# Graph attention on one core: one-hots, transposes and their copies made two groups ahead of the products instead of one

## The chip, the cores and the metric

The kernel runs on one core of a Trainium2 chip. The metric is the time on the device in microseconds (us); the median of three runs is given, and one further execution was profiled. A group below is four tiles of 128 edges each, a window is eight groups.

## The reference

One layer of graph attention over 6250 nodes and 206250 edges, which come sorted by receiver, then a residual and a layer norm:

```python
sent = nodes[senders] @ Ws + Ws_b
e_att = sent + edges @ We + We_b
recv = nodes[receivers] @ Wr + Wr_b
logits = einsum('ehd,do->eho', mish(e_att + recv), attn_w) + attn_b
seg_max = segment_max(logits, receivers)
w = exp(logits - seg_max[receivers])
w = w / segment_sum(w, receivers)[receivers]
out_nodes = segment_sum(w * e_att, receivers)
x = layernorm(x + out_nodes)
```

There are 4 heads of 32, so 128 features. All data are float32.

## The kernel before

The edges are cut into W = 51 windows of 4096 (128 partitions times T = 32 tiles). In a window the receivers span at most 128 nodes, so a sum over receivers is a matrix product with a one-hot of 128 columns. Tables of the nodes' sender and receiver projections are made first and stored to DRAM. Then each engine runs its own loop over windows and, in them, over NG = 8 groups of GT = 4 tiles. The windows from 2 to 49 are a loop of two windows a turn; two buffers (b) hold the data of even and odd windows.

For group g of window w:

- VectorE, `one_hots` (L1073): the one-hot of the group's local receivers (L1077). It writes the buffer of two windows back, so it waits for the sums of the same group of window w-2 (L1075).
- TensorE, `turn` (L761): four transposes of the edges (L768) into the one PSUM tile `ps_edgeT` and four of the one-hot, as bf16 (L773), into the one `ps_onehotT`. The first wait for ScalarE's copy of the group before (L766), the second for `one_hots` and that copy's pair (L770, L771).
- ScalarE, `copy_edgeT` (L878, L883) and `copy_onehotT` (L885, L890): copies of the two to SBUF, into one of two buffers (g % 2), each after the products of two groups back.
- TensorE, `products` (L777): for each tile edges times We (L787) plus one-hot times the receivers' rows (L788), added up in `ps_z`, 16 instructions a group, since a float32 matmul is two. They wait for both copies and for the addition of two groups back.
- GpSimd, `gathers` (L693, L699): for each tile an indirect DMA that fetches 128 rows of the senders' table, 4 a group. Those of a group start when the addition of the group four back is done (AHEAD = 4, L697).
- VectorE, `add_gathered` (L1082, L1088): products plus gathered rows into Z, "the addition". Then `clamp` (L1096); ScalarE's four steps exp, square, ln, exp (L897, L900, L903, L907); and on VectorE, a group later, `mish` (L1103), `score` (L1112) and `reduce_heads` (L1118), which give the logits.

When a window's logits are there, its maxima are found in the next window (L1121 to L1168), the weights are made, `messages` (L1174, L1179) multiplies them into Z, and `sums` on TensorE (L792, L799) adds up the messages over receivers with the one-hots as stationary operand, eight instructions a group. The tables MSG_NEXT, MSG_LAST (messages) and SUM_NEXT, SUM_LAST (sums) say in which group of the next or next but one window each is issued: SUM_NEXT = {5: [0], 6: [1], 7: [2]} in the next, SUM_LAST = {1: [3, 4], 2: [5, 6], 3: [7]} in the one after it. `attended`, `moments` and `normalise` finish a window two windows later and SyncE stores it. `prepare` (L1052) makes the local receivers (part 1, L1057, L1059) and the penalties (part 2) of the next window in group 6.

The engines run independently and each in its own order. In a group g VectorE does: one-hots of g+1, addition of g, messages, clamp of g, mish, score and reduction of g-1, and small work between them. TensorE does: products of g, transposes of g+1, sums. ScalarE does: copies of g+1, the four steps of g. SyncE, in order: edge load, receivers, receiver indices, sender indices (after the gathers), store and residual rows of finished windows; the edge load waits for the last edge transposes of two windows back (L607).

Of the kernel before, what the change touches and what calls it, by code (L numbers as in the profile page):

```python
# [51 lines left out]
SUM_NEXT = {5: [0], 6: [1], 7: [2]}  # L52
SUM_LAST = {1: [3, 4], 2: [5, 6], 3: [7]}
NCONST = 3
# [13 lines left out]
def gat_kernel(nc, x, src, dst, edges, ws_k, ws_b, wr_k, wr_b, we_k, we_b, attn_w, attn_b, out):  # L68
# [13 lines left out]
    with ctx:  # L82
# [217 lines left out]
        def after(w, b, g):  # L300

            return (w, b, g + 1) if g + 1 < NG else (w + 1, 1 - b, 0)

        def before(w, b, g):
            return (w, b, g - 1) if g else (w - 1, 1 - b, NG - 1)

        def run(eng, window):

            window(0, 0, 0)
            window(1, 1, 0)  # L310
            with eng.Fori(1, W // 2) as i:
                window(i * 2, 0, i)
                window(i * 2 + 1, 1, i)
            window(W - 1, 0, W // 2)
            window(W, 1, W // 2)
            window(W + 1, 0, W // 2 + 1)
# [403 lines left out]
        def _(pe):  # L720
# [96 lines left out]
            def window(w, b, k):  # L817
                for g in range(NG):
                    if there(w):
                        products(w, b, k, g)  # L820
                    w1, b1, g1 = after(w, b, g)
                    if there(w1) and there(w):
# [12 lines left out]
            pe.wait_ge(s_xs, 2 * NB)  # L835
            turn(0, 0, 0, 0)
            run(pe, window)
            pe.wait_ge(fin, (W - 1) * FIN)
# [7 lines left out]
        def _(act):  # L846
# [82 lines left out]
            def window(w, b, k):  # L929
                for g in range(NG):  # L930
                    w1, b1, g1 = after(w, b, g)
                    here, coming = there(w), there(w1) and there(w)
# [16 lines left out]

            copy_edgeT(0, 0, 0)  # L950
            copy_onehotT(0, 0, 0)
            run(act, window)
# [4 lines left out]
        def _(dve):  # L957
# [279 lines left out]
            def aside(w, b, k, g, part):  # L1237

                if g == 3 and there(w - 1):
                    subtract_maxima(w - 1, 1 - b, part)  # L1240
                if g == 4 and there(w - 2):
                    attended(w - 2, b, k - 1, part)
                if g == 5 and there(w - 2):
                    moments(w - 2, b, k - 1, part)
                if g == 6 and there(w + 1) and there(w):
                    prepare(w + 1, 1 - b, k + b if b else k, part)
# [7 lines left out]
            def window(w, b, k):  # L1254


                for g in range(NG):
                    w1, b1, g1 = after(w, b, g)
                    w0, b0, g0 = before(w, b, g)
# [32 lines left out]
            dve.wait_ge(prep_row, 1)  # L1292
            one_hots(0, 0, 0)
            look_for_unsorted()
            run(dve, window)
# [25 lines left out]
```

## Time and profile before

| what | value |
|---|---|
| median of three runs | 2827.16 us (2823.28 to 2833.03) |
| profiled execution | 2829.57 us, its span 2827.6 us |
| mean granted clock of TensorE | 0.848 |
| instructions in the span | 45501 |
| mean DMA rate | 85 GB/s |

The profile's page gives the busy time of each engine, the idle time before each group of instructions and what ended it. "Remote" in it means that the semaphore that ended a wait rose at a moment near which no recorded instruction of the program ended; the kernel runs on one core, so it is no other core. "Issue" is idle time in which an engine waited for nothing that the profile shows. The granted clock is a share of 2.4 GHz; it has two levels here, 0.50 and 1.00.

### The profile page before, as it was taken

What the parts mean: (1) busy time and instruction counts of PE and PEld (TensorE: products, weight loads), DVE (VectorE), ACT (ScalarE), POOL (GpSimd) and SP (SyncE); (2) the same over time, 40 slices, a digit from 0 to 9 for tenths busy, and PEclk for the clock granted to TensorE, in tenths of its full rate; (3) what the DMA queues carried; (4) which work ended last, traced back from release to release, by engine and by line L of the source; (5) the groups of instructions that cost most, each with busy time, mean ns of one, the idle gap of its engine ahead of it and who ended that gap; (6) DMA issues with size and microseconds to landing.
All of it is one profiled execution on the core that took longest, in us unless ns stands there. A gap on an engine that the chain in (4) does not pass through costs nothing.

```text
span 2827.6 us, 45501 instructions
## 1 busy us (share of the span) xinstructions
PE 1930.7 (68%) x13618; PEld 1782.6 (63%) x13618; DVE 2032.6 (72%) x4348; ACT 1634.8 (58%) x2717; POOL 1555.1 (55%) x1640
## 2 busy tenths in 40 slices
PE   4566777667676676676667676677666666767666
PEld 4566666666666666666666666666566666666665
DVE  3577777777777777767777777777777677777776
ACT  1556555556565665565655656655656556656663
POOL 2555555555555555555555555555555555555551
PEclk9788788888888888888887988888988789888888
DMA  6322322322322322232232232232232232232220
GB/s 198 105 71 75 107 74 74 107 73 73 108 71 73 99 82 72 77 101 73 75 104 75 75 105 75 76 104 75 75 105 74 72 106 73 73 103 76 74 77 17
DMA packets 107468, 240.30 MB, mean 85 GB/s; under 512 B 46429, under 2 KB 73300, under 8 KB 100412
## 3 DMA queue, kind: packets, MB, share of 16 engines
q0 software_dynamic: 52224, 107.06, 14.4%
q1 hardware_dynamic: 53074, 132.41, 13.7%
q10 hardware_dynamic: 2142, 0.49, 0.1%
q8 instruction: 13, 0.21, 0.0%
q14 instruction: 15, 0.12, 0.0%
HBM read 230.09 MB, written 9.74 MB: 85 GB/s over the span
## 4 chain that ended last, share of the span: by engine, by line
DVE 35%; PE 24%; another core or an unknown queue 18%; issue 16%; ACT 4%; DVEq 1%; ACTq 1%; SPq 0%; DMA 0%
PE ps_z L787 7%; PE ps_z L788 7%; DVE tbuf L1112 6%; DVE Z L1088 5%; DVE tbuf L1103 5%; DVE onehot L1077 5%; PE ps_sum L799 4%; DVE Z L1179 4%; DVE tbuf L1096 3%; DVE logit L1118 2%; PE ps_onehotT L773 2%; PE ps_edgeT L768 1%; ACT tbuf L900 1%; ACT tbuf L897 1%
## 5 line engine op out<-in xcount | busy, mean ns | idle before, releaser
L699 POOL DMA_INDIRECT gath<-xs_table,src_i x1632 | 1554.2, 952 | 1218.6 <-DVE Z L1088 652.5
L787 PE MATMUL ps_z<-we_sb,edgeT 128*128 128x128 f32 x3264 | 800.3, 334 | 575.2 <-ACT edgeT L883 316.5
L787 PEld LDWEIGHTS ps_z<-we_sb,edgeT 128*128 128x128 f32 x3264 | 622.6, 237 | 629.2 <-ACT edgeT L883 345.7
L788 PE MATMUL ps_z<-xr_buf,onehotT 128*128 128x128 f32 x3264 | 768.6, 324 | 4.2 <-issue 4.2
L1088 DVE TENSOR_TENSOR Z<-ps_z,gath 128x512 f32<-128x512 f32 x408 | 279.9, 686 | 553.5 <-remote 399.4
L788 PEld LDWEIGHTS ps_z<-xr_buf,onehotT 128*128 128x128 f32 x3264 | 630.5, 240 | 4.1 <-issue 4.1
L883 ACT COPY edgeT<-ps_edgeT 128x512 f32<-128x512 f32 x408 | 238.4, 584 | 668.6 <-remote 463.7
L799 PE MATMUL ps_sum<-Z,onehot 128*128 128x132 f32 x3264 | 491.1, 300 | 37.6 <-issue 32.7
L799 PEld LDWEIGHTS ps_sum<-Z,onehot 128*128 128x128 f32 x3264 | 440.9, 209 | 42.1 <-issue 37.3
L890 ACT CAST onehotT<-ps_onehotT 128x512 f32<-128x512 bf16 x408 | 239.7, 588 | 199.7 <-remote 135.3
L1077 DVE TENSOR_TENSOR onehot<-iota_f,ps_dve 128x512 f32<-128x512 f32 x408 | 272.8, 669 | 100.3 <-remote 100.3
L897 ACT ACTIVATE tbuf<-tbuf 128x512 f32<-128x512 f32 x408 | 257.8, 632 | 123.9 <-DVE tbuf L1096 80.4
L773 PE MATMUL ps_onehotT<-ident_half,onehot 128*128 128x128 bf16 x1632 | 180.3, 238 | 212.1 <-DVE onehot L1077 126.2
L768 PE MATMUL ps_edgeT<-ident,edge_buf 128*128 128x128 f32 x1632 | 296.5, 308 | 27.1 <-issue 20.9
L900 ACT ACTIVATE tbuf<-tbuf,c_one 128x512 f32<-128x512 f32 x408 | 294.6, 722 | 13.3
L903 ACT ACTIVATE tbuf<-tbuf,c_one 128x512 f32<-128x512 f32 x408 | 294.6, 722 | 13.3
L773 PEld LDWEIGHTS ps_onehotT<-ident_half,onehot 128*128 128x128 bf16 x1632 | 118.6, 107 | 283.9 <-DVE onehot L1077 167.8
L907 ACT ACTIVATE ps_ratio<-tbuf,c_ln 128x512 f32<-128x512 f32 x408 | 281.3, 689 | 17.1 <-ACT tbuf L903 2.1
L1112 DVE TENSOR_TENSOR tbuf<-tbuf,ps_dve 128x512 f32<-128x512 f32 x408 | 278.4, 682 | 7.3
L1118 DVE TENSOR_REDUCE logit<-tbuf 128x16 f32<-128x512 f32 x408 | 277.7, 681 | 7.3
L1103 DVE SCALAR_TENSOR_TENSOR tbuf<-ps_ratio,Z 128x512 f32<-128x512 f32 x408 | 277.7, 681 | 0.0
L1179 DVE TENSOR_TENSOR Z<-Z,ps_dve 128x512 f32<-128x512 f32 x408 | 272.1, 678 | 1.8
(107 smaller groups left out, 1131.0 us busy)
## 6 DMA issues: line engine op xcount, KB each, us to landing
edge_buf<-in_edge_attr_dram SPq DMA_DIRECT2D x51, 2048.0 KB
gath<-xs_table,src_i POOLq DMA_INDIRECT x1632
xr_buf<-xr_table SPq DMA_DIRECT2D x51, 64.0 KB
xr_in<-xr_table SPq DMA_DIRECT2D x51, 64.0 KB
x_in<-in_x_dram SPq DMA_DIRECT2D x51, 64.0 KB
out_dram<-y_out SPq DMA_DIRECT2D x51, 64.0 KB
xs_table<-onehot SPq DMA_DIRECT2D x2, 896.0 KB
xr_table<-Z SPq DMA_DIRECT2D x1, 1568.0 KB
```

What stands on the lines that cost most here:

```text
L699: nc.gpsimd.indirect_dma_start(gath[:, b, t, :], None, xs_dram, bass.IndirectOffsetOnAxis(ap=src_i[:, b, t:t + 1], axis=0))\
L768: tr = nc.tensor.transpose(ps_edgeT[:, j, :], edge_buf[:, b, a + j, :], ident[:, :])
L773: tr = nc.tensor.transpose(ps_onehotT[:, j, :].bitcast(BF16)[:, 0:P], halves(OHv[:, b, a + j, :]), ident_half[:, :])
L787: nc.tensor.matmul(ps_z[q][:, j, :], edgeT[:, q, j, :], we_sb[:, :], start=True, stop=False)
L788: mm = nc.tensor.matmul(ps_z[q][:, j, :], onehotT[:, q, j, :], xr_buf[:, b, :], start=False, stop=True)
L799: mm = nc.tensor.matmul(ps_sum[:, 0:ZC], OHv[:, b, t, :], Zv[:, b, t, :], start=(t == 0), stop=(t == T - 1))
L1077: nc.vector.tensor_tensor(OHv[:, b, a:a + n, :], iota_f[:, :].unsqueeze(1).to_broadcast([P, n, P]), local[:, b, a:a + n].unsqueeze(2).to_b ...
L1088: nc.vector.tensor_tensor(Zv[:, b, a:a + n, 0:D], ps_z[g % 2][:, 0:n, :], gath[:, b, a:a + n, :], ALU.add).then_inc(z_ready, 1)
L1103: nc.vector.scalar_tensor_tensor(out=tb, in0=ratio, scalar=1.0, in1=Zv[:, b, a:a + n, 0:D], op0=ALU.subtract, op1=ALU.mult, reverse0=True)\
L1112: nc.vector.tensor_tensor(tb, tb, row.to_broadcast([P, n, D]), ALU.mult).then_inc(scored, 1)
L1118: nc.vector.tensor_reduce(logit[:, b, :, a:a + n].rearrange("p h t -> p t h"), tb, AX.X, ALU.add)\
L1179: nc.vector.tensor_tensor(zz, zz, ww, ALU.mult).then_inc(msg_ready, 1)
```

## The change

One-hots, transposes and copies are issued for the group two ahead of the products: `two_after` takes the place of `after` on VectorE, TensorE and ScalarE, and a second group of each is made before the loop. The sums of the window two back move one group sooner: 3 and 4 to group 0, 5 to group 1, 6 to group 2; 7 stays in group 3. Part 1 of `prepare` moves from group 6 to group 5, since the one-hots of the next window's first group now come at the head of group 6. Buffers, GpSimd and SyncE are as before.

```diff
-SUM_LAST = {1: [3, 4], 2: [5, 6], 3: [7]}
+SUM_LAST = {0: [3, 4], 1: [5], 2: [6], 3: [7]}
...
+        def two_after(w, b, g):
+
+            return after(*after(w, b, g))
+
...
                 for g in range(NG):
                     if there(w):
                         products(w, b, k, g)
-                    w1, b1, g1 = after(w, b, g)
+                    w1, b1, g1 = two_after(w, b, g)
                     if there(w1) and there(w):
                         turn(w1, b1, k if w1 is w else (k + b if b else k), g1)
...
             turn(0, 0, 0, 0)
+            turn(0, 0, 0, 1)
             run(pe, window)
...
                 for g in range(NG):
-                    w1, b1, g1 = after(w, b, g)
+                    w1, b1, g1 = two_after(w, b, g)
                     here, coming = there(w), there(w1) and there(w)
                     if coming:
                         copy_edgeT(w1, b1, g1)
...
-            copy_edgeT(0, 0, 0)
-            copy_onehotT(0, 0, 0)
+            for g in range(2):
+                copy_edgeT(0, 0, g)
+                copy_onehotT(0, 0, g)
...
-                if g == 6 and there(w + 1) and there(w):
+                if (g, part) in ((5, 1), (6, 2)) and there(w + 1) and there(w):
                     prepare(w + 1, 1 - b, k + b if b else k, part)
...
-                    w1, b1, g1 = after(w, b, g)
+                    w1, b1, g1 = two_after(w, b, g)
                     w0, b0, g0 = before(w, b, g)
                     if there(w1) and there(w):
                         one_hots(w1, b1, g1)
...
             one_hots(0, 0, 0)
+            one_hots(0, 0, 1)
             look_for_unsorted()
```

## Rows read from the trace of the kernel before

**Rows 1.** The page, part 1: busy us, share of the span, instructions

```profile
PE 1930.7 (68%) x13618; PEld 1782.6 (63%) x13618; DVE 2032.6 (72%) x4348; ACT 1634.8 (58%) x2717; POOL 1555.1 (55%) x1640
```

**Rows 2.** The addition's line: ns min/median/max, first and last start

```profile
L1088 DVE TENSOR_TENSOR Z<-ps_z,gath x408: 671/691/693, 78.0 to 2789.5; 128x512 f32<-128x512 f32 x136
```

**Rows 3.** Table of waits: who <- what ended it: us, times, longest

```profile
DVE Z L1088 <- remote: 399.4, 137, 4.9
...
PE ps_z L787 <- ACT edgeT L883: 316.5, 119, 5.1
...
DVE Z L1088 <- PE ps_z L788: 143.4, 66, 7.2
...
DVE onehot L1077 <- remote: 100.3, 28, 4.0
```

**Rows 4.** Timeline of TensorE's matmuls: start, us, line, names, count [idle before]

```profile
1398.65 1.12 PE L799 MATMUL ps_sum<-Z,onehot 128*128 128x132 f32 x8
1399.61 0.39 PE L787 MATMUL ps_z<-we_sb,edgeT 128*128 128x128 f32 x2
...
1401.17 0.39 PE L788 MATMUL ps_z<-xr_buf,onehotT 128*128 128x128 f32 x2
...
1406.65 0.35 PE L799 MATMUL ps_sum<-Z,onehot 128*128 128x132 f32 x1 [0.45 <-issue]
1408.34 0.77 PE L787 MATMUL ps_z<-we_sb,edgeT 128*128 128x128 f32 x2 [1.34 <-ACT onehotT L890]
```

**Rows 5.** Timeline of VectorE and ScalarE from the anchor at 1406.80

```profile
1406.80 0.69 DVE L1088 TENSOR_TENSOR Z<-ps_z,gath 128x512 f32<-128x512 f32 x1 [3.71 <-remote]
1406.93 0.59 ACT L883 COPY edgeT<-ps_edgeT 128x512 f32<-128x512 f32 x1 [3.68 <-remote]
...
1410.63 0.68 DVE L1077 TENSOR_TENSOR onehot<-iota_f,ps_dve 128x512 f32<-128x512 f32 x1
...
1412.13 0.69 DVE L1088 TENSOR_TENSOR Z<-ps_z,gath 128x512 f32<-128x512 f32 x1 [0.83 <-issue]
...
1416.92 0.59 ACT L890 CAST onehotT<-ps_onehotT 128x512 f32<-128x512 bf16 x1 [3.34 <-remote]
...
1421.06 0.69 DVE L1088 TENSOR_TENSOR Z<-ps_z,gath 128x512 f32<-128x512 f32 x1 [3.44 <-PE ps_z L788]
```

**Rows 6.** Timeline of GpSimd: eight gathers and the first of the next

```profile
1395.17 0.97 POOL L699 DMA_INDIRECT gath<-xs_table,src_i  x1 [3.24 <-DVE Z L1088]
...
1404.07 0.94 POOL L699 DMA_INDIRECT gath<-xs_table,src_i  x1 [0.30 <-issue]
1408.27 0.96 POOL L699 DMA_INDIRECT gath<-xs_table,src_i  x1 [3.25 <-DVE Z L1088]
```

**Rows 7.** Timeline of VectorE: a one-hot's wait at group 2, and anchors

```profile
1143.56 0.69 DVE L1088 TENSOR_TENSOR Z<-ps_z,gath 128x512 f32<-128x512 f32 x1 [3.96 <-remote]
...
1156.59 0.69 DVE L1077 TENSOR_TENSOR onehot<-iota_f,ps_dve 128x512 f32<-128x512 f32 x1 [3.96 <-remote]
1157.19 0.68 DVE L1088 TENSOR_TENSOR Z<-ps_z,gath 128x512 f32<-128x512 f32 x1
...
1164.42 0.69 DVE L1088 TENSOR_TENSOR Z<-ps_z,gath 128x512 f32<-128x512 f32 x1 [1.23 <-PE ps_z L788]
...
1393.69 0.69 DVE L1088 TENSOR_TENSOR Z<-ps_z,gath 128x512 f32<-128x512 f32 x1 [2.30 <-PE ps_z L788]
```

**Rows 8.** Stretch of products, busy us of PE, PEld, DVE, ACT, POOL; clock, DMA

```profile
1408.30:1412.10 3.80, 3.76 (x17) 3.79 (x18) 2.94 (x6) 2.77 (x4) 2.88 (x4) 0.50 0.16 43
```

**Rows 9.** Groups by line: names, count | busy us, mean ns | idle before

```profile
L1077 DVE TENSOR_TENSOR onehot<-iota_f,ps_dve 128x512 f32<-128x512 f32 x408 | 272.8, 669 | 100.3 <-remote 100.3
...
L1103 DVE SCALAR_TENSOR_TENSOR tbuf<-ps_ratio,Z 128x512 f32<-128x512 f32 x408 | 277.7, 681 | 0.0
...
L1096 DVE TENSOR_SCALAR tbuf<-Z 128x512 f32<-128x512 f32 x408 | 179.7, 440 | 2.1
```

**Rows 10.** Timeline of VectorE: the first operation of prepare, part 1

```profile
1400.41 0.24 DVE L1057 TENSOR_SCALAR ps_dve<-dst_i,base_f 128x32 f32<-128x32 int32 x1
```

**Rows 11.** SyncE's own waits: line <- what: us, times, longest

```profile
SPq L294 <- DVE y_out L1225: 244.5, 10, 45.3
```

## What I expect, and why

> **What bounds the kernel now.** I read the page first. No engine is full: VectorE 2032.6 us of a span of 2827.6, TensorE 1930.7, ScalarE 1634.8, GpSimd 1555.1 [rows 1]. Per group of four tiles (408 of them) that is 4.98, 4.73, 4.01 and 3.81 us, while a group takes 6.66 us: the additions into Z run from 78.0 to 2789.5, 407 steps in 2711.5 us [rows 2]. So the kernel is bound by waits, and the table of waits says which: VectorE's additions for "remote" (399.4 us) and for the products (143.4), TensorE's products for ScalarE's copies (316.5), VectorE's one-hots for "remote" (100.3) [rows 3]. "Remote" on one core means here that a semaphore rose and no instruction of the program had its recorded end near that moment.
>
> The timeline shows what it is. The products of the group that is added at 1406.80 have their last record from 1401.17 for 0.39 us [rows 4]; the addition that needs only them and a long landed gather starts at 1406.80 after 3.71 us idle, and ScalarE's copy of the transposes behind those products at 1406.93, after 3.68 [rows 5]. TensorE's results become known to others about 5 us after their record. GpSimd's timeline gives the pattern [rows 6]: the addition at 1393.69 lets gathers start at 1395.17; eight are issued, until 1405.01, and 1.79 us later the held results come free. 1.48 + 9.84 + 1.79 = 13.11 us, the distance of the additions at 1393.69 [rows 7] and 1406.80 [rows 5]. The first addition of such a cycle frees four gathers, the second one four more, the third is held until they are through. So the basic loop is VectorE's addition, eight gathers, TensorE's held update, and it does two groups in 13.1 us: 6.55 each. I call the additions that end a hold anchors.
>
> Here a page speaks against reading this as a hold. The Trainium skill, "Perfetto Trace Analysis", section "Per-engine timelines", says that TensorE's end time is computed by the profiler from an instruction's size and not observed. By it TensorE could really be computing until 1406.7, its bound would be its own work, and reordering would bring nothing; that is the rival "nothing moves" below. The trace leaves it open, though the last sum before 1406.8 stands alone behind 0.45 us of idle for nothing the profile shows [rows 4], which fits a TensorE that is stopped more than one that works.
>
> **The change part by part.** No instruction is added or removed: 408 one-hots, pairs of copies and sets of transposes stay. They move.
>
> 1. *Copies two groups ahead.* Now TensorE's order is products(g), transposes(g+1), sums, products(g+1), and products(g+1) stand behind ScalarE's copies of g+1: 2 x 0.59 us and, after an anchor, a start at 1408.34 where the addition was at 1406.80 [rows 4, 5]. Then they run at a granted clock of 0.50, the 1.2 GHz level, and last until the next addition at 1412.13 [rows 5, 8], 3.8 us and 5.33 after the anchor; those from 1399.61 to 1401.56 took 2.0 [rows 4]. After the change products(g+1) have their copies from a group before. Their other wait (Z two back) is unchanged, and copy(g+2) now waits for products(g), which stand ahead of its transposes anyway: nothing. But the gain is capped: VectorE comes to the second addition by itself about 4.4 us after the first (wide operations of 0.68 and a clamp of 0.44 [rows 9]; the one-hot starts 3.83 after the anchor and takes 0.67 at most, 1410.63 against 1406.80 [rows 5]), and the second four gathers cannot start before the first four are issued, 1.48 + 10.1/2 = 6.5 after the anchor. At a regular anchor the gain is 0; what can be gained is where the second addition comes too late and GpSimd's eight break into four and four, as from 1157.19 to 1164.42, 7.23 us for one group [rows 7], or where copies are themselves held, as that of 1416.92 with the addition then at 1421.06 behind 3.44 us idle [rows 5].
>  The whole that irregular cycles cost is 2711.5 - 407 x 6.55 = 45.6 us. Ends: 0 and 45.6 gained.
>
> 2. *The wait at group 2.* VectorE's one-hot of group 3 stands at the head of group 2, and needs the sums of the same group two windows back, which TensorE makes in group 1, only one group earlier. They fall into the hold: 28 one-hots waited, 100.3 us [rows 3]. The price is not 100: at 1156.59 the one-hot waited 3.96 us and the addition followed at 1157.19 with no wait [rows 7]; without it the addition itself would have waited to 1156.6. So 0.60 each, 28 x 0.60 = 17 us, part of the 45.6. With the new table these sums come in group 0: gone.
>
> 3. *New waits of the same kind.* This is what speaks against the change. One-hots now stand two groups ahead. Counting which group makes the sum and which needs it (one-hots of 0, 1 at groups 6, 7 and of 2, 3 at groups 0, 1; sums 0, 1, 2 at 5, 6, 7, sum 3 at 0): the distance is one group at four places, 6, 7, 0 and 1, where now it is one at group 2 alone. The other four have two. In the windows from 1143 to 1412 five anchors at these places wait 3.7 us or more for a held update, of 20 places (first 1143.56, last 1406.80, five in all) [rows 5, 7]. 5/20 x 204 = 51 new events at 0.60 = 31 us. A sum that is done before the hold costs 0 (lower end); all places twice per window and with a broken pair behind each (7.23 against 6.55 per group, 0.68) is 102 x 1.28 = 131 (upper end). I take 31, the row of the same wait.
>  Who stands behind such a wait: on VectorE the addition; on TensorE the onehot transposes, and behind them, in order, the sums and the products that were to run ahead. At these anchors part 1 brings nothing.
>
> 4. *Sums one group sooner.* Each is eight instructions in 1.12 us [rows 4]. Their messages are made at least one group ahead in both tables, so they wait for nothing new. Groups 1 and 2 held two each; now group 0 holds two and the others one: moved, 0, between plus and minus one sum (1.12) at an anchor, within part 3's ends.
>
> 5. *prepare, part 1, at group 5* instead of 6: two small operations, the larger 0.24 us [rows 10], moved, 0; at an anchor they lie in its wait, elsewhere they would cost up to 0.5 x 51 = 24. At the start one more one-hot stands ahead of the search, 0.67 us [rows 9]: 0 to 0.7.
>
> 6. *SyncE's queue.* The 2 MB edge load waits for the last edge transposes of two windows back, which come a group sooner. It is held by the store ahead of it, which waits for the normalised rows (244.5 us on that) [rows 11], so it does not move: 0. If it moved a group (6.6 us) it would meet other gathers; bounds plus and minus 3 us a window where it shows, which I leave to the range.
>
> **Sum.** 2829.6 (the profiled execution; its span is 2827.6) - 45.6 + 31 = 2815. The median of the three runs is 2827.2, 2.4 below it, so 2813 to 2815; I say 2814, 0.5% faster. I take the whole 45.6 because the two things that are seen to break cycles, late products and the wait at group 2, are what the change moves.
>
> **The rivals.**
> - *The new waits win* (slower). Mechanism: at 6, 7, 0 and 1 the one-hot waits for held sums, TensorE stands behind it and goes on at the lower clock, and the next products come so late that the eight gathers break into four and four. For: the same wait at group 2 did just that: 1156.59, then 1157.19 to 1164.42 [rows 7]. Against: only group 0 has two sums ahead of the products. Price 1.28 each; with no gain of part 1 but the 17 of part 2, 51 events give 2827 + 65 - 17 = 2875; with half the gain of part 1, 2860; with a third of the places, 2840. Middle 2850. It decides from 45.6 / 1.28 = 36 events on, where each costs the full price.
> - *Nothing moves*. The loop of addition, eight gathers and held update contains none of the moved parts; or TensorE really works until the update. Then 2827 plus or minus 8.
> - *Three groups fit into a cycle*: with products ahead, the third addition is known before the hold begins, and twelve gathers follow each other. (1.48 + 14.9 + 1.79) / 3 = 6.06 a group, 0.5 less; in a third of the 407 steps that is 67 us: 2760. Against: TensorE waits with the transposes of g+3 for a one-hot that VectorE starts 3.83 us after the anchor, and only behind them and a sum come the products of g+2: 3.83 + 0.67 + 0.2 + 1.12 + 2.0 = 7.8 us after it [rows 4, 5], when the record of the hold of 1406.80 had long begun (its products ended 1401.56, 7.9 after 1393.69).
> - *The change does not reach its distance*: TensorE still stops at the edge transposes of g+2 until the copy of g+1 has freed the one buffer. It is part of "nothing moves".
>
> **How the numbers follow.** Forecast (2795 to 2820) 0.38; new waits win 0.34; nothing moves 0.22; three groups 0.06. The range should leave out 2 in 10: it takes the forecast, nothing moves, and the slower case to 2868, and down to 2770: **2770 to 2868**. The likeliest case's own range is 2795 to 2820. A measurement here tells 0.3% (8.5 us) from no change. Faster by more than that 0.42, within 0.22, slower 0.36.
>
> **What would show it.** Right: the additions of regular anchors still 13.1 apart; the idle time of the one-hots for "remote" no longer at group 2 but at 6, 7, 0 and 1, some 50 times; TensorE's products waiting for the copy of edgeT far less than 316.5 us; the additions' wait for ps_z below 143.4. Wrong: one-hots with over 70 such waits, more pairs 7.2 apart, or bursts of twelve gathers (faster). The sum is wrong at its root if the hold is no matter of the gathers: then anchors would not come 1.8 us behind the last gather's issue.

## The result, and the profile after

The kernel after takes 2771.8 us (median of 4 runs, 2766.4 to 2773.1), the kernel before beside it 2830.1 (4 runs, 2823.3 to 2839.2): ratio 0.9763, 95% interval 0.9728 to 0.9797. That is 2.4% faster. The forecast was 2814 us, 0.5% faster; the direction was right, the size was not: of the 58 us gained, 13 were foreseen (2827.2 to 2814), under a quarter. The time lies 2 us inside the stated range of 2770 to 2868, and outside 2795 to 2820, the likeliest case's own. The profiled execution has a span of 2764.5 us at a granted clock of 0.866.

The page's part 1 of the kernel after:

```profile
PE 1889.1 (68%) x13618; PEld 1751.4 (63%) x13618; DVE 2027.6 (73%) x4348; ACT 1631.1 (59%) x2717; POOL 1570.5 (57%) x1640
```

The busy times are those of before [rows 1] within 16 us, TensorE aside (42 less, at a slightly higher clock). The kernel is still bound by waits. The tables of waits of VectorE, TensorE and GpSimd (who <- what ended it: us, times, longest), and the line of the addition with its first and last start:

```profile
DVE Z L1094 <- remote: 620.9, 199, 5.7
...
DVE Z L1094 <- PE ps_z L792: 14.9, 17, 3.8
...
DVE onehot L1083 <- remote: 7.4, 4, 4.0
...
PE ps_onehotT L777 <- DVE onehot L1083: 357.8, 180, 4.0
PE ps_onehotT L777 <- issue: 265.6, 125, 5.1
PE ps_sum L803 <- issue: 92.1, 141, 1.7
...
POOL gath L703 <- DVE Z L1094: 659.7, 208, 10.4
...
L1094 DVE TENSOR_TENSOR Z<-ps_z,gath x408: 659/691/693, 76.9 to 2728.7; 128x512 f32<-128x512 f32 x136
```

Against [rows 3]: the products' wait for ScalarE's copies, 316.5 us, is gone; so are the additions' waits for products (143.4, now 14.9) and the one-hots' (100.3, now 7.4). What came in their place is the hold itself: additions wait for "remote" 199 times where they did 137 times, that is at nearly every second of the 408 groups. GpSimd's timeline tells what that means for its bursts (gathers with less than 1 us between them): 196 are of eight, 3 of four and 3 of twelve; of the kernel before 152 were of eight and 100 of four. Nearly every cycle is now the regular pair.

The arithmetic closes. The additions run 2728.7 - 76.9 = 2651.8 us, where they ran 2711.5 [rows 2]: 59.7 less; what lies outside took 116.1 and takes 112.7: 3.4 less; together the 63.1 between the spans.

A regular cycle of the kernel after on VectorE (timeline, one-hots and additions):

```profile
1363.44 0.69 DVE L1094 TENSOR_TENSOR Z<-ps_z,gath 128x512 f32<-128x512 f32 x1 [3.01 <-remote]
...
1367.69 0.66 DVE L1083 TENSOR_TENSOR onehot<-iota_f,ps_dve 128x512 f32<-128x512 f32 x1
1368.27 0.68 DVE L1094 TENSOR_TENSOR Z<-ps_z,gath 128x512 f32<-128x512 f32 x1
...
1372.28 0.68 DVE L1083 TENSOR_TENSOR onehot<-iota_f,ps_dve 128x512 f32<-128x512 f32 x1
1376.41 0.69 DVE L1094 TENSOR_TENSOR Z<-ps_z,gath 128x512 f32<-128x512 f32 x1 [3.45 <-remote]
...
1380.24 0.68 DVE L1083 TENSOR_TENSOR onehot<-iota_f,ps_dve 128x512 f32<-128x512 f32 x1
```

The additions of 1363.44 (group 5) and 1376.41 (group 7) end holds, 12.97 apart; the one between needs no wait, since its products had their copies a group before. GpSimd's first gather of the cycle is at 1364.92 and the eighth ends at 1374.72. TensorE in the same cycle (timeline of matmuls):

```profile
1368.41 0.40 PE L777 MATMUL ps_onehotT<-ident_half,onehot 128*128 128x128 bf16 x4 [3.02 <-DVE onehot L1083]
1368.64 1.12 PE L803 MATMUL ps_sum<-Z,onehot 128*128 128x132 f32 x8
1369.60 0.38 PE L791 MATMUL ps_z<-we_sb,edgeT 128*128 128x128 f32 x2
...
1371.16 0.39 PE L792 MATMUL ps_z<-xr_buf,onehotT 128*128 128x128 f32 x2
...
1374.21 0.27 PE L791 MATMUL ps_z<-we_sb,edgeT 128*128 128x128 f32 x1
1374.88 0.35 PE L791 MATMUL ps_z<-we_sb,edgeT 128*128 128x128 f32 x1 [0.40 <-issue]
1376.28 0.39 PE L792 MATMUL ps_z<-xr_buf,onehotT 128*128 128x128 f32 x2 [1.05 <-issue]
```

Two things are to be seen. The sum that the one-hot of 1372.28 needs is made from 1368.64, directly behind the transposes, 4.8 us after the burst's first gather when it ends; it was known in time. The products behind it, recorded until 1371.55, 6.6 us after it, were not: their addition is that of 1376.41. And behind 1374.21 TensorE has one product at a time with idle time for "issue" between them, until the hold ends at 1376.4: it does not only tell late what it has done, it is itself stopped. All sixteen records of that group's products are in the trace, so no missing record fills the gaps.

### The profile page after: what moved, and what is told of

Read it like the earlier page. It is cut to its first block, busy times and chain, and to the rows that moved or that the text cites. A ratio compares the mean times of both kernels' runs of the same rounds, so it can differ in the third digit from the quotient of the medians.

```text
span 2764.5 us, 45477 instructions
## 1 busy us (share of the span) xinstructions
PE 1889.1 (68%) x13618; PEld 1751.4 (63%) x13618; DVE 2027.6 (73%) x4348; ACT 1631.1 (59%) x2717; POOL 1570.5 (57%) x1640
## 3 DMA queue, kind: packets, MB, share of 16 engines
q0 software_dynamic: 52224, 107.06, 14.9%
## 4 chain that ended last, share of the span: by engine, by line
DVE 51%; another core or an unknown queue 21%; issue 16%; PE 9%; DVEq 1%; ACTq 1%; ACT 1%
DVE Z L1094 8%; DVE onehot L1083 8%; DVE tbuf L1118 8%; DVE tbuf L1109 7%; DVE Z L1185 6%; DVE tbuf L1102 4%; DVE logit L1124 3%; PE ps_sum L803 3%; PE ps_z L791 2%; PE ps_z L792 2%; DVE ends_max L1159 1%; DVE item_pen L1145 1%; PE ps_onehotT L777 1%; PE ps_edgeT L772 1%
## 5 line engine op out<-in xcount | busy, mean ns | idle before, releaser
L791 PE MATMUL ps_z<-we_sb,edgeT 128*128 128x128 f32 x3264 | 760.5, 319 | 38.3 <-issue 37.7
L792 PE MATMUL ps_z<-xr_buf,onehotT 128*128 128x128 f32 x3264 | 744.0, 313 | 47.1 <-issue 46.7
L791 PEld LDWEIGHTS ps_z<-we_sb,edgeT 128*128 128x128 f32 x3264 | 608.3, 231 | 52.9 <-issue 49.9
L803 PE MATMUL ps_sum<-Z,onehot 128*128 128x132 f32 x3264 | 571.0, 323 | 100.7 <-issue 92.1
L792 PEld LDWEIGHTS ps_z<-xr_buf,onehotT 128*128 128x128 f32 x3264 | 604.1, 229 | 54.7 <-issue 53.2
L777 PE MATMUL ps_onehotT<-ident_half,onehot 128*128 128x128 bf16 x1632 | 171.4, 231 | 630.8 <-DVE onehot L1083 357.8
L803 PEld LDWEIGHTS ps_sum<-Z,onehot 128*128 128x128 f32 x3264 | 493.2, 226 | 118.0 <-issue 109.5
L777 PEld LDWEIGHTS ps_onehotT<-ident_half,onehot 128*128 128x128 bf16 x1632 | 105.7, 102 | 708.9 <-DVE onehot L1083 404.6
L912 ACT ACTIVATE ps_ratio<-tbuf,c_ln 128x512 f32<-128x512 f32 x408 | 281.2, 689 | 11.6
L772 PE MATMUL ps_edgeT<-ident,edge_buf 128*128 128x128 f32 x1632 | 261.7, 285 | 18.5 <-issue 12.7
```

Source lines behind the costliest of these rows:

```text
L777: tr = nc.tensor.transpose(ps_onehotT[:, j, :].bitcast(BF16)[:, 0:P], halves(OHv[:, b, a + j, :]), ident_half[:, :])
L791: nc.tensor.matmul(ps_z[q][:, j, :], edgeT[:, q, j, :], we_sb[:, :], start=True, stop=False)
L792: mm = nc.tensor.matmul(ps_z[q][:, j, :], onehotT[:, q, j, :], xr_buf[:, b, :], start=False, stop=True)
L803: mm = nc.tensor.matmul(ps_sum[:, 0:ZC], OHv[:, b, t, :], Zv[:, b, t, :], start=(t == 0), stop=(t == T - 1))
```

## The experiments

The runs were made in five sets, each with the kernel before beside it on the same chip. The kernel before took 2829.7 us in the first, 2184.9 in the second, 2186.4 in the third, 2759.8 in the fourth and 2847.6 in the fifth. All ratios are within a set. Each set ran on another chip and no chip was used twice, so a difference between sets can be one of the chip or of the moment; "chip" below stands for both.

**Set 1: the parts, and the gathers.** The sums' table alone, in the kernel before:

```diff
-SUM_LAST = {1: [3, 4], 2: [5, 6], 3: [7]}
+SUM_LAST = {0: [3, 4], 1: [5], 2: [6], 3: [7]}
```

> The kernel before with the new table of sums alone (3 and 4 in group 0, 5 in 1, 6 in 2). Theory A (the gain is that broken cycles became regular, and the wait of the one-hot at group 2 was what broke them): the 28 one-hot waits go, most of the 100 bursts of four gathers with them, and the time falls by 40 us or more, to 2790 or less. Theory B (it takes the greater distance of transposes and copies): the 28 waits of 0.60 us go, 17 us at most, 2810 to 2825, and bursts of four stay at 70 or more.

Measured: 2809.0 us, ratio 0.9928 (0.9894 to 0.9961). No one-hot waited, and GpSimd's timeline has 80 bursts of four instead of 100. That is theory B, 1 us below its bounds.

The kernel after with transposes and copies one group ahead as before:

```diff
-                    w1, b1, g1 = two_after(w, b, g)
+                    w1, b1, g1 = after(w, b, g)
...
-            turn(0, 0, 0, 1)
...
-            for g in range(2):
-                copy_edgeT(0, 0, g)
-                copy_onehotT(0, 0, g)
+            copy_edgeT(0, 0, 0)
+            copy_onehotT(0, 0, 0)
...
```

> The changed kernel with transposes and copies one group ahead again; one-hots stay two ahead, the sums in the new table. Theory A (VectorE's earlier one-hots free TensorE's transposes): as the changed kernel, 2765 to 2780, nearly all bursts of eight. Theory B (products must not stand behind ScalarE's copies of the group before): between the two, 2800 to 2830, TensorE's products still wait 200 us or more for the copy of edgeT.

Measured: 2828.2 us, ratio 1.0004 (0.9972 to 1.0036), theory B. Here are the waits that the prediction feared (table of waits, and VectorE's timeline):

```profile
DVE onehot L1081 <- remote: 315.3, 92, 4.7
...
PE ps_z L791 <- ACT edgeT L887: 219.6, 100, 5.1
...
1350.06 0.69 DVE L1081 TENSOR_TENSOR onehot<-iota_f,ps_dve 128x512 f32<-128x512 f32 x1 [4.01 <-remote]
1350.66 0.68 DVE L1092 TENSOR_TENSOR Z<-ps_z,gath 128x512 f32<-128x512 f32 x1
```

92 one-hots waited, all of groups 0 to 3 (made at groups 6, 7, 0 and 1), nearly twice the 51 forecast. With the copies' distance they are 4. So the parts do not add: the sums alone bring 21 us (11 to 30), one-hots and sums together nothing, and with the copies it was 58 in the first comparison. The copies' distance is what makes the earlier one-hots harmless.

Half the gathers, in the kernel before and in the kernel after: from the third window on only two of a group's four tiles are gathered, the other two keep what an earlier window left there, so the work of half the gathers is left out. The waits for landed gathers are halved to match.

```diff
-                    for t in range(a, a + n):
+                    few = n if isinstance(w, int) and w < 2 else n // 2
+                    for t in range(a, a + few):
...
```

> The kernel before with two gathers a group in place of four from the third window on (tiles 2 and 3 of a group add rows that an earlier window left). Theory of the held updates (the loop is addition, gathers, TensorE's updates set free when the gathers are through): the loop of two groups shrinks from 13.1 us to 1.5 + 5.0 + 1.5, 8 us, under VectorE's own 5.0 a group, so 2150 to 2400 us in all, VectorE bound. Rival (TensorE really computes until its late updates): no less work for TensorE, 2800 to 2830.

> The changed kernel with two gathers a group in place of four from the third window on (tiles 2 and 3 of a group add rows that an earlier window left). Held updates: VectorE bound, 2100 to 2350 us, and ahead of the kernel before with half its gathers by 50 us or more, since copies no longer stand between products. Rival (TensorE really computes): 2760 to 2775.

Measured: 2208.9 and 2211.4 us, ratios 0.782 and 0.783. TensorE, VectorE and ScalarE do the same work as ever, in 78% of the time. From the windows with half the gathers on, no addition waits for "remote" in either; the few that do start before 162 us, while four gathers a group are still made. So the loop that sets the time goes through the gathers. The second half of the last expectation failed: the change, said to be 50 us ahead here, is worth nothing, so its gain shows only where updates are held.

**Sets 2 and 3: the same kernels where nothing is held.** Four variants of the kernel after were to follow the cycle. An idle operation of GpSimd ahead of each group's gathers (128 columns); one of 512 columns with the gathers six groups ahead instead of four; the last sums one group apart from their one-hots; one-hots three groups ahead, behind the clamp:

```diff
...
+                    nc.gpsimd.iota(pad_i[:, :], pattern=[[1, 128]], base=0, channel_multiplier=0).then_inc(s_pad, 1)
...
```
```diff
-AHEAD = 4
+AHEAD = 6
...
+                    nc.gpsimd.iota(pad_i[:, :], pattern=[[1, 512]], base=0, channel_multiplier=0).then_inc(s_pad, 1)
```
```diff
-SUM_LAST = {0: [3, 4], 1: [5], 2: [6], 3: [7]}
+SUM_LAST = {0: [3], 1: [4], 2: [5, 6], 3: [7]}
```
```diff
-SUM_NEXT = {5: [0], 6: [1], 7: [2]}
-SUM_LAST = {0: [3, 4], 1: [5], 2: [6], 3: [7]}
+SUM_NEXT = {5: [0], 6: [1], 7: [2, 3]}
+SUM_LAST = {0: [4], 1: [5], 2: [6], 3: [7]}
...
-                if (g, part) in ((5, 1), (6, 2)) and there(w + 1) and there(w):
+                if (g, part) in ((4, 1), (6, 2)) and there(w + 1) and there(w):
...
-                    w1, b1, g1 = two_after(w, b, g)
+                    w1, b1, g1 = after(*two_after(w, b, g))
...
-                    if there(w1) and there(w):
-                        one_hots(w1, b1, g1)
...
+                    if there(w1) and there(w):
+                        one_hots(w1, b1, g1)
...
```

> The changed kernel with one small operation on GpSimd (an iota of 128 columns, 0.23 us in the profile of the kernel before, at L690) ahead of each group's four gathers. If the loop is addition, eight gathers, late updates, each of the 204 pairs gets two of them, 0.5 us at the least and 1.1 with 0.3 us of issue each: 2870 to 2990. If TensorE's own work were the bound, GpSimd has 40% idle and nothing moves: 2760 to 2780.

> The changed kernel with gathers up to six groups ahead and an iota of 512 columns (about 0.5 to 0.9 us) on GpSimd ahead of each group's four, so that no eight gathers run without a break. If a break of over 1 us each group is enough to let TensorE's updates through: 5.0 + 1.1 to 1.4 us a group, 2600 to 2720. If the engine must be idle for longer, or counts as busy in the iota: 13.1 + 2 x 0.8 us for two groups, 2900 to 3060.

> The changed kernel with the sums of the window two back as late as they can be: 3 in group 0, 4 in 1, 5 and 6 in 2, 7 in 3. The one-hots of groups 4 and 5 then also stand only one group behind their sums (six places of eight in place of four). The prediction's step 3 (a one-hot one group behind its sum meets a held update and costs 0.60 us): 30 to 60 us slower than the changed kernel, 2800 to 2830. If the regular cycle keeps the sums out of the held stretch, as the profile of the changed kernel shows with 7.4 us of such waits: within 8 us of it.

> The changed kernel with the one-hots three groups ahead, made behind the clamp, sum 3 in group 7 of the next window and 4 in group 0. TensorE's transposes then never wait for a one-hot, and the products two groups behind an anchor can be done 4 to 5.5 us after it, before updates are held. If that is what keeps a third group out of a cycle: many bursts of twelve gathers, 6.1 to 6.4 us a group, 2600 to 2730 us. If updates are held whatever is ready: 2760 to 2790.

Measured, in that order: 2214.8, 2338.4, 2171.6 and 2163.6 us; ratios 1.0136, 1.0699, 0.9929 and 0.9891, each within 0.002. None of the expected numbers could come, because the kernel before took 2184.9 us in this set: no addition waited for "remote" in any of the four. As tests of the held cycle they are void. The two with idle operations show something else, though. GpSimd's timeline of the first:

```profile
1362.46 0.94 POOL L708 DMA_INDIRECT gath<-xs_table,src_i  x1 [0.30 <-issue]
1363.40 0.26 POOL L706 IOTA pad_i<- 128x128 int32 x1
1363.82 0.95 POOL L708 DMA_INDIRECT gath<-xs_table,src_i  x1 [0.16 <-POOL pad_i L706]
```

From the fifth group on neither has a single pause of GpSimd longer than the 0.30 us of issue, over 1616 gathers. Gathers are 1.25 us apart; with the idle operation between them it is 1.36 in the first and 1.69 in the second (1364.99 to 1366.68), 0.11 and 0.44 more, over some 404 groups 44 and 178 us. Beside the three-ahead kernel of the same set, which has no pause of GpSimd either, they take 51 and 175 us more. What is added to GpSimd there comes out as time: where nothing is held, GpSimd's issuing sets the pace of these kernels.

So the change itself and three variants were run again, with an expectation for either case:

> The changed kernel itself, beside the kernel before, since the second set of runs found the kernel before at 2184.9 us where the first set had 2829.7: there no addition waited for "remote" and VectorE was busy for 93% of the span. Theory A (what the change is worth hangs on held TensorE updates): where the kernel before is near 2830, 2765 to 2780, ratio 0.976; where it is near 2185, the ratio is 0.993 to 1.003, 2170 to 2192, since VectorE's own work of 2025 us is the bound and only the products' wait for copies goes. Theory B (the change brings 2.4% by an order that is better anywhere): ratio 0.976 in both places, 2132 us beside 2185.

> One-hots and sums as in the change, transposes and copies one group ahead as before. In the first set this had 92 one-hots that waited (315 us idle) and was no faster than before, 2828.2. Theory A (it is held sums that make the one-hots wait): where the kernel before takes 2185, no one-hot waits (under 10 us), and the time is 2178 to 2195; where it takes 2830, 2820 to 2836 again. Theory B (the one-hots wait because TensorE's own order brings the sums too late): some 90 one-hots wait in both places, and it is over 2215 where the kernel before takes 2185.

> The changed kernel with its last sums at groups 0: 3, 1: 4, 2: 5 and 6, 3: 7, where the change has 0: 3 and 4, 1: 5, 2: 6, 3: 7. Sum 4 stands one group before the one-hot that needs it again, as in the kernel with new one-hots and old copies; only one sum stands ahead of the products at group 0. Theory A (with the copies two ahead, TensorE works early enough that every sum is known before a hold begins, so a one-hot does not wait): where the kernel before takes 2830, 2765 to 2785 and under 15 us idle of one-hots; where it takes 2185, 2168 to 2174. Theory B (the sums' table decides about the waits): over 30 one-hots wait, 2790 to 2820 where the kernel before takes 2830.

> The changed kernel with the one-hots three groups ahead (made behind the clamp), transposes and copies two ahead as in the change, sum 3 of a block one group sooner (in group 7 of the window after) and the first part of the preparation at group 4. Theory A (the held loop of addition, eight gathers, update takes 13.1 us and nothing in VectorE's order can shorten it): where the kernel before takes 2830, 2755 to 2785, the same as the change; where it takes 2185, 2158 to 2165 as measured before (2163.6). Theory B (the one-hot's place between hold and addition costs after each anchor, 0.67 us in 204 cycles, at least a fifth of it): under 2745 where the kernel before takes 2830.

The kernel before took 2186.4. Measured: the change 2187.4, ratio 1.0005 (0.9996 to 1.0015); one-hots and sums only 2167.0, 0.9915 (0.9898 to 0.9932); sums one apart 2170.4, 0.9927 (0.9910 to 0.9945); three ahead 2165.3, 0.9913 (0.9895 to 0.9931). For the change that is theory A, and for one-hots and sums only too as to the waits (none), though it is 11 us faster than its bounds; the other two came at theory A's times (three ahead at the upper bound). The change's page, part 1 and VectorE's row of busy tenths, then waits of VectorE, TensorE and GpSimd:

```profile
PE 1629.2 (75%) x13618; PEld 1523.9 (70%) x13618; DVE 2025.0 (93%) x4348; ACT 1634.0 (75%) x2717; POOL 1569.1 (72%) x1640
...
DVE  3799999999999999999999999999999999999997
```
```profile
DVE ends_max L1159 <- PE ps_ends L818: 58.3, 50, 1.8
...
DVE Z L1094 <- PE ps_z L792: 17.8, 21, 11.2
...
PE ps_onehotT L777 <- DVE onehot L1083: 500.2, 362, 3.4
...
POOL gath L703 <- issue: 472.3, 1538, 0.9
...
POOL gath L703 <- DVE Z L1094: 47.6, 93, 6.9
```

VectorE is busy for 93%, and GpSimd hardly pauses: its 72% leave out the 0.30 us of issue behind each gather, and among its last 1616 gathers only 29 pauses are longer than 0.45 us, 16 us in all beyond the issue. A group takes 5.09 us (2073.2 us of additions in 407 steps), four gathers 5.0. "Remote" is gone, and so are TensorE's idle times for "issue", of which the kernel after had 265.6 and 92.1 us at its transposes and sums where updates were held. GpSimd's gathers take what they took there, 962 and 961 ns each. The same program is bound by held updates on one chip and by GpSimd's and VectorE's own pace on another, 600 us apart, and the change is worth 2.4% on the first and nothing on the second. There the copies' distance even costs: the variant without it is 20 us faster. Its own waits:

```profile
POOL gath L703 <- issue: 472.7, 1551, 0.3
DVE Z L1092 <- DMA gath<-xs_table,src_i: 54.8, 47, 3.5
```

GpSimd has no pause left at all, and additions wait for gathers to land. VectorE's wait of `ends_max` for TensorE, 58.3 us in the change, is 1.0 here, and its busy time 2011.2 instead of 2025.0 (the clamp 176.6, 187.5). It would fit that these waits of VectorE make the 29 pauses in the change; no run tests it.

**Set 4: again with holds.** The three-ahead kernel and the one with sums one apart, as above:

> The same kernel as the one with one-hots three groups ahead, made behind the clamp, again: wanted is a set of runs in which the kernel before takes 2830. Theory A (what is lost after a hold is lost between the anchor's addition and the next one; the one-hot ahead of the second addition is 0.67 us of the 4.3 to 4.5 there, but the second four gathers can't start before the first four are issued, 6.2 us after the anchor): 2755 to 2785 there, additions of a regular cycle 13.0 to 13.2 apart. Theory B (sums and one-hots now fall into one group, and a sum made over 2 us after the burst's first gather is known only behind it, so the one-hot behind the clamp waits for it and with it the message and the scores): 2790 to 2850 there. Where the kernel before takes 2185: 2160 to 2168 again.

> The same kernel as the one with the last sums at 0: 3, 1: 4, 2: 5 and 6, 3: 7, again, for a set in which the kernel before takes 2830. Theory A (in the change anchors stand at groups 1, 3, 5, 7; a one-hot of an even group comes behind an addition that ended a hold, when everything is known, and one of an odd group needs a sum made just behind the one-hot of the group before, in the first 2 us of the burst, which are not held): this table moves only sum 4, needed at an even group, so no one-hot waits (under 15 us idle) and it takes 2765 to 2785. Theory B (one group between sum and one-hot is too little in general, and the change's table avoids it by luck of the place): over 30 one-hots wait, 2790 to 2820. Where the kernel before takes 2185: 2167 to 2174 again.

The kernel before took 2759.8. Three ahead: 2783.8, ratio 1.0091 (1.0075 to 1.0108). The bounds had been set for 2830; as ratios theory A's are 0.973 to 0.984 and theory B's 0.986 to 1.007, so it is B, and worse. One apart: 2733.3, ratio 0.9910 (0.9894 to 0.9927): no one-hot waited, as theory A has it, but the ratio is not within A's (0.977 to 0.984); it is within B's (0.986 to 0.996), for which over 30 one-hots were to wait. Neither theory holds whole. Here the held cycle is shorter (bursts of eight start 12.92 apart, 13.08 in the kernel after at first) and the kernel before loses less; the change itself was not run in this set. The table of waits of three ahead and one of its one-hots, with TensorE at the time:

```profile
DVE onehot L1083 <- remote: 220.5, 38, 7.8
...
1390.78 0.69 DVE L1083 TENSOR_TENSOR onehot<-iota_f,ps_dve 128x512 f32<-128x512 f32 x1 [7.68 <-remote]
```
```profile
1382.11 0.41 PE L791 MATMUL ps_z<-we_sb,edgeT 128*128 128x128 f32 x2
1382.99 0.27 PE L792 MATMUL ps_z<-xr_buf,onehotT 128*128 128x128 f32 x1 [0.47 <-issue]
1383.72 0.35 PE L792 MATMUL ps_z<-xr_buf,onehotT 128*128 128x128 f32 x1 [0.46 <-issue]
1385.80 0.27 PE L791 MATMUL ps_z<-we_sb,edgeT 128*128 128x128 f32 x1 [1.74 <-issue]
```

TensorE's two sums ahead of these products are recorded until 1381.38; the one-hot that needs one of them waited until 1390.78, 9.4 us after that. An order among the fastest where nothing is held (0.9891 and 0.9913) loses where updates are held.

**Set 5: a sum pushed into the hold.** The change itself; the change with twelve products of a zero matrix ahead of the sums of group 0; the same twelve behind them; and sums one apart, as in sets 2 to 4.

```diff
+                    if g == 0 and there(w - 2):
+                        for _ in range(12):
+                            nc.tensor.matmul(ps_sum[:, 0:P], zeros[:, :], ident[:, :], start=False, stop=False)
                     for m in SUM_LAST.get(g, []) if there(w - 2) else []:
                         sums(w - 2, b, m)
...
```

> The changed kernel, beside the two with idle products below and the table of sums one apart, so that all four stand on one chip. Both theories: on a chip that holds TensorE's updates, ratio 0.97 to 0.99 to the kernel before, with under 15 us idle of one-hots; where nothing is held, 1.000.

> The changed kernel with twelve products of a zero matrix added to the running sum, by TensorE in group 0 of each window, ahead of sums 3 and 4. The work grows by 12 x 51 products of some 0.14 to 0.3 us each, 1.7 us or more per window, in an engine that is idle 3 us per hold. In the change sum 3 was made 4.5 us (median) after a burst's first gather and known at once in 42 of 44 windows; updates 5 to 10 us after it are held. Theory A (the one-hots of odd groups don't wait because their sum is made just before the hold bites): where updates are held, sum 3 now falls into the hold and the one-hot at group 1 waits 3 to 4 us in most of 49 windows, 150 us or more in all; the addition follows 0.6 later at least: 30 to 60 us slower than the change. Theory B (the one-hots have room, the place of the sum in the cycle doesn't matter): within 8 us of the change. Where nothing is held: within 15 us of it.

> The same twelve idle products, but behind sums 3 and 4 of group 0: the same work in the same group, and sum 3 is as early as in the change. Theory A: no one-hot waits (under 15 us idle); the products of group 1 are 1.7 us or more later and are held anyway: within 8 us of the change. Theory B: the same time as the kernel with the idle products ahead of the sums, since only TensorE's work counts.

> The changed kernel with the last sums at 0: 3, 1: 4, 2: 5 and 6, 3: 7, beside the change itself: it moves one sum (about 1.1 us) out of group 0 and sum 6 stays in group 2. Theory A (the held cycle is addition, eight gathers, update, whatever stands in group 0): within 8 us of the change where updates are held. Theory B (fewer instructions ahead of the products of an anchor group bring its message and preparation sooner, as where nothing is held, 2170 beside 2187): 10 us or more faster than the change in both places.

Beside 2847.6 of before: the change 2780.6, ratio 0.9762 (0.9740 to 0.9785), as at first; idle ahead 2872.1, 1.0088 (1.0065 to 1.0111); idle behind 2883.7, 1.0123 (1.0096 to 1.0149); one apart 2774.4, 0.9738 (0.9717 to 0.9759).

The waits went as theory A has it (tables of waits, first of idle ahead, then of idle behind):

```profile
DVE Z L1101 <- remote: 453.5, 154, 6.4
DVE onehot L1090 <- remote: 175.4, 54, 4.3
DVE Z L1101 <- PE ps_z L794: 60.0, 53, 4.7
```
```profile
DVE Z L1101 <- remote: 432.4, 150, 6.3
DVE Z L1101 <- PE ps_z L794: 231.5, 58, 6.3
DVE onehot L1090 <- remote: 36.8, 17, 4.4
```

With the idle products ahead of sum 3 the one-hot that needs it waited over 1 us in 42 of 51 windows, behind it in 5. But theory A's times failed: the kernel with 37 more waits is the faster of the two by 11.6 us, and both are 91 and 103 slower than the change. A one-hot's wait inside a hold has, by this pair, no price that can be seen; the pair is no clean measure of it, since with the idle products behind the sums the additions wait 231.5 us for products, and 60.0 with them ahead. Theory B, the same time for both, is near, 11.6 us off, but has no place for the 42 waits. What has a price is TensorE's work in that group:

```profile
1378.23 1.73 PE L834 MATMUL ps_sum<-ident,zeros 128*128 128x128 f32 x14
1380.36 0.36 PE L834 MATMUL ps_sum<-ident,zeros 128*128 128x128 f32 x1 [0.40 <-issue]
1381.80 0.35 PE L834 MATMUL ps_sum<-ident,zeros 128*128 128x128 f32 x1 [1.08 <-issue]
1383.91 0.27 PE L834 MATMUL ps_sum<-ident,zeros 128*128 128x128 f32 x1 [1.76 <-issue]
1384.66 1.51 PE L834 MATMUL ps_sum<-ident,zeros 128*128 128x128 f32 x7 [0.48 <-issue]
1385.96 0.64 PE L793 MATMUL ps_z<-we_sb,edgeT 128*128 128x128 f32 x2
...
1384.74 0.69 DVE L1090 TENSOR_TENSOR onehot<-iota_f,ps_dve 128x512 f32<-128x512 f32 x1 [3.83 <-remote]
1389.14 0.69 DVE L1101 TENSOR_TENSOR Z<-ps_z,gath 128x512 f32<-128x512 f32 x1 [3.71 <-PE ps_z L794]
```

These are TensorE's and VectorE's timelines of the kernel with the idle products behind the sums; the twelve are 24 records (x). They wait for no semaphore. Between 1379.96 and 1384.66 TensorE does three records; then the rest at once, when the hold ends and the held one-hot starts too (1384.74). The products of group 1 come behind them, from 1385.96, and their addition waits for them until 1389.14; a one-hot's 0.60 after the hold's end it would have been 1385.3. What TensorE has not done when the hold begins, it does after it.

## Why the prediction was right or wrong

- **The loop** (addition, eight gathers, held update) stands where updates are held: 13.11 us was read, 13.08 is the median after, 12.97 in the cycle shown. With half the gathers the hold is gone, and with it over a fifth of the time. What the prediction took for an update that is told late is also an engine that is stopped.
- **Step 1, copies two ahead: the mechanism was right, the size too small.** Forecast 45.6 us with step 2 in it, the upper end; the loop lost 59.7. The 45.6 rest on 6.55 for half of 13.11; with 6.555 it is 43.6. Of the 14 more, 204 cycles at 13.08 instead of 13.11 are 6; the few bursts of twelve are part of the rest.
- **Step 2, the wait at group 2: right**, and measured by itself: 17 us forecast, 21 measured with the table alone (11 to 30 by its interval), which has no one-hot that waits.
- **Step 3, 51 new waits at 0.60, 31 us: this step failed.** There were 4, 7.4 us in all. The count was taken from the places where anchors stood in the kernel before, five of twenty, as if each anchor at such a place had the one-hot's wait ahead of it. (The whole trace has 37 additions there that waited 3.7 us or more for "remote", not 51, so by its own rule the term was 22.) In the regular cycle anchors stand at the odd groups. A one-hot of an even group (1380.24) comes behind an addition that ended a hold, when all is known; one of an odd group (1372.28) needs a sum that TensorE makes right behind the even group's transposes (1368.64), before it is stopped. The step counted events in the old pattern after step 1 had changed the pattern. Its own mechanism is real: without the copies' distance there were 92 waits, and with a sum pushed behind idle products 42 in one place alone. That part 1 "brings nothing" at such places was wrong in the same way. Its price of 0.60 found no support either: in set 5 the kernel with 37 waits more is the faster one, though the two differ in more than those waits.
- **Step 4, sums sooner: 0 within one sum per window.** Moving one sum out of group 0 gave 6.2 us (2780.6 to 2774.4), of overlapping intervals; but twelve idle products there cost 91 to 103. TensorE's idle time in the hold, which the expectations of set 5 counted on, is no cover: TensorE is stopped in it.
- **Steps 5 and 6** can't be told apart from nothing; outside the loop 3.4 us went.
- **The rivals.** "The new waits win" fell: the waits did not come. "Three groups fit" is 3 bursts of twelve, not a third. "The change does not reach its distance" fell: the products' wait for copies is gone. "Nothing moves" was right in set 3 (1.0005), for a reason that no rival had: nothing is held there. Its form from the Trainium skill, "Perfetto Trace Analysis", section "Per-engine timelines" (TensorE's end is an estimate, so it may really be computing), does not hold here: the same matmuls fit into 2183 us elsewhere, and in the hold there are 0.4 to 1.8 us of idle between starts of ones that wait for nothing. That rests on starts, which the page does not call estimated.
- **Of the signs named in advance** the distance of anchors, the copies' wait and the additions' wait came as for "right"; the one-hots' 50 waits did not.

Sum corrected: 2829.6 - 59.7 - 3.4 = 2766.5, the profiled execution's time. Had step 3 been 0, the sum would have been 2784. Of the 48 us between its 2815 and the 2766.4 measured, 31 are step 3, 14 the size of step 1 and 3 lie outside the loop. That the range held the result at all is owed to its width, not to the sum.

What stays open: why the updates are held in the first comparison and in sets 1, 4 and 5 and not in sets 2 and 3, whether that belongs to the chip or to the moment, and what holds TensorE. The runs show that it comes with eight gathers issued in a row (from between 4.8 and 6.6 us after the first to 1.7 after the last, in the cycle shown), and that it goes when half of them are left out; not what is shared. Whether a gap between the gathers would let TensorE on was the question of the two idle operations of GpSimd, and they were not run where updates are held.

## What to carry to other kernels

If a cycle of waits sets the time, count new waits in the cycle as it will be after the change, not at the places of the old trace: a part that regularises the cycle moves all of them. Then test a change on more than one chip: the one-apart table (0.9929, 0.9927, 0.9910, 0.9738) is faster than the kernel before in every set, by under 1% in three of them, the change only where updates are held, and three ahead is 0.9 to 1.1% better in two sets and 0.9% worse in a third. Add the issue time to an engine's busy time before calling it free: GpSimd at 72% was full. And an engine that seems idle in a hold is no cover until something independent has been seen to run there.

## What the runs showed of the hardware

- The same kernel took 2185, 2186, 2760, 2830 and 2848 us in five sets of runs, each on another chip, while repetitions within a set lie at most 1.1% apart. GpSimd's gathers cost the same in all: 0.95 to 0.97 us busy and 0.30 for issue, 1.25 from start to start. Where nothing was held, that pace set the time: 0.11 and 0.44 us more a group on GpSimd came out as 51 and 175 us.
- In three of the sets and in the first comparison, what TensorE finished in the second half of eight indirect gathers became known only behind them (products recorded until 1371.55, addition at 1376.41; in a burst of twelve a sum 9.4 us late), and TensorE itself started one matmul record in 0.7 to 2.1 us there, with no semaphore between them. Where nothing was held, the kernel with the change has no idle time of TensorE for "issue" among its waits, with the same gathers at the same pace.
- Where updates were held, twelve idle 128 x 128 products per window cost 1.8 and 2.0 us per window (91 / 51, 103 / 51) on an engine that is busy for 68% of the span.
